# Attention layers on one core: the Sync engine's order, with the read-back of q and k behind the second row of maxima

## Chip, core and metric

The kernel runs on one core of a Trainium2 chip. The metric is the device time of one launch in microseconds (us). TensorE is the matrix engine (PE; PEld is its weight load), VectorE is DVE, ScalarE is ACT, GpSimd is POOL, and SyncE is SP (SPq in the trace: its instruction queue), which here only issues DMAs.

## What is computed

Two layers, each: group norm of x (64 samples of 14 x 14 tokens and 192 channels, 32 groups), then attention with 12 heads of 16 channels and a relative position bias that depends on q, then a projection, added to x.

```python
x = x + _L0_conv_ref(_gn(x), ...)
x = x + _L1_conv_ref(_gn(x), ...)
# each layer, with B = 64 samples, nh = 12, hd = 16, HW = 196:
qkv = hidden.reshape(B, HW, C) @ W + b
attn = einsum('bqd,bkd->bqk', q * scale, k)
rel_h = einsum('bhwc,hkc->bhwk', q, Rh)
rel_w = einsum('bhwc,wkc->bhwk', q, Rw)
attn = softmax(attn + rel_h[..., None] + rel_w[..., None, :])
out = einsum('bqk,bkd->bqd', attn, v) @ proj + b
```

## The kernel before

One sample of one layer is a unit; there are 128 (2 x 64). The kernel is one software pipeline over units. Every engine runs the same loop: iteration i has 12 slots, and a table gives each piece of work a number "at". A piece with number `at` belongs, in iteration i, to unit i - at // 12 and stands in slot at % 12. Within a slot the order is that of the code. The tables are `JOBS` (TensorE's jobs), `POOL_AT` and `SP_AT`; `due` (with `head_at` for the heads) picks the unit. A number therefore sets two things: the unit lag, and the place in the engine's instruction order. All waits are semaphore waits ahead of the instruction, so an engine's queue stands still behind one that waits.

Per unit: x is loaded (xa), transposed, normalised, q, k and v are made (jobs qk0, qk1 in slot 3, v in slot 10). q and k go in two halves (high and low part in f16) to DRAM (L341, `to_dram`) and are read back in another layout: q to q_st (L369), k to k_st in two DMAs (L375). q_st and k_st hold a stack of rows over which one matmul contracts: q and k rows, rows of the relative bias (rel_hl, written by four DMAs of L358), and one last row with minus the maximum of each query. For that row, TensorE first computes all scores once (L525, into ps_max), VectorE reduces them to maxima (L722), TensorE transposes six heads' maxima at a time (jobs mT0, mT1), ScalarE copies them to mrow (L610), and a DMA of the Sync engine puts each half into the last row of q_st (L336, `maxima`; half 0 is called m0, half 1 m1). Then the scores are computed again with the row in them (L538, into ps_sc; head 0 needs m0, head 6 needs m1), ScalarE takes the exponential, the product with v follows (L557, with the sum of the softmax in it), then the transposition, division and projection. ScalarE makes yr from the projection (L657), GpSimd adds the input (L862: yo = yr + xd), and the Sync engine writes it out (L387). xd is loaded by the Sync engine (L382).

The heads' scores: `MAX_AT` is 28 and `EXP_AT` is 40, one head a slot. So head 0 of the second scores stands in slot 4, head 6 in slot 10. The transposition mT0 is at 35 (slot 11), mT1 at 41 (slot 5); ScalarE copies mrow one slot later (slots 0 and 6). The relative bias is made by jobs rel0 to rel2 at 17, 18 and 20. GpSimd's `POOL_AT` has mv at -11 (slot 1) ahead of y at 63 (slot 3), and mv waits for VectorE's statistics, which stand in slot 5.

The Sync engine's order in one iteration, from `SP_AT` before: slot 0 xa (L394); slot 3 m0 (L336), q and k to DRAM (L341 twice, waits for VectorE's low part of q and k), q read back (L369, waits until q has landed in DRAM); slot 4 k read back (L375 twice, waits until k has landed); slot 7 xd (L382, waits for the yo of the unit before its own); slot 9 output (L387, waits for its own yo); slot 10 m1 (L336, waits for mrow) and the relative bias (L358 four times, waits for VectorE's rel_hl, L776).

```python
wait(sp, s_mrow, unit_.n * 2 + half + 1)   # maxima: m0, m1
wait_dma(sp, s_qd, u)                      # q_in
wait_dma(sp, s_kd, u)                      # k_in
wait(sp, s_y, u.n - 1)                     # xd
wait(sp, s_y, u.n + 1)                     # out
```

Of the kernel before, what the change touches and what calls it, by code (L numbers as in the profile page):

```python
# [71 lines left out]
def attention_kernel(nc, x_in, w_all, b_qk, b_rows, rel, onehot, lo_rows, ident_in, gmat_in, out):  # L72
    with ExitStack() as ctx:
# [41 lines left out]
        def pair(name, shape, dt=F32):  # L115
            return [sb(f"{name}{i}", shape, dt) for i in range(2)]

        xa = pair("xa", [HT, 2, C])
# [25 lines left out]
        xd = pair("xd", [HT, 2, C])  # L144
# [126 lines left out]
        POOL_AT = {"mv": -11, "group": -3, "xn": -1, "xhi": 0, "xlo": 0, "y": 63}  # L271
        QK_TILES = ((0, 1), (2,))

        SP_AT = {"m0": 39, "m1": 46, "rel": 22, "qk_out": 3, "q_in": 3, "k_in": 4, "xd": 55, "out": 69, "xa": -12}

        def head_at(base, slot):

# [2 lines left out]
        def due(unit, slot, at):  # L280

            u = unit(at // HEADS)
            return u if at % HEADS == slot and active(u) else None
# [24 lines left out]
        def _(sp):  # L308
# [23 lines left out]
            def maxima(unit_, half):  # L332

                if active(unit_):
                    wait(sp, s_mrow, unit_.n * 2 + half + 1)
                    sp.dma_start(q_st[unit_.r][R_MAX:STACK, half * HH:half * HH + HH, :, :],  # L336
                                 mrow[unit_.r % 2][:, half, :]).then_inc(s_m[half][unit_.r], 16)

            def to_dram(unit_, dram, row, landed):

                sp.dma_start(dram[unit_.r].rearrange("l d h c t -> (d h) l (c t)"),  # L341
                             qk_hl[unit_.r % 2][row:row + HQ * HD, :, :, :]
                             .rearrange("p l c t -> p l (c t)")).then_inc(landed[unit_.r], 16)

            def iteration(unit, layer):
                for s in range(HEADS):
                    for half in range(2):
                        u = due(unit, s, SP_AT[f"m{half}"])
                        if u:
                            maxima(u, half)  # L350
                    u = due(unit, s, SP_AT["rel"])
                    if u:
                        wait(sp, s_rlo, u.n * 3 + 3)
                        for axis in range(2):
                            rows = RW if axis == 0 else 2 * SIDE
                            for half in range(2):
                                p, r0 = 64 * axis + 32 * half, R_REL + RW * axis
                                sp.dma_start(q_st[u.r][r0:r0 + rows, half * HH:half * HH + HH, :, :],  # L358
                                             rel_hl[u.r % 2][p:p + rows, :, :]).then_inc(s_rel[u.r], 16)
                    u = due(unit, s, SP_AT["qk_out"])  # L360
                    if u:
                        wait(sp, s_qklo, u.n * 2 + 2)
                        to_dram(u, q_dram, 0, s_qd)
                        to_dram(u, k_dram, HQ * HD, s_kd)
                    u = due(unit, s, SP_AT["q_in"])
                    if u:
# [3 lines left out]
                          .then_inc(s_qst[u.r], 16)  # L370
                    u = due(unit, s, SP_AT["k_in"])
                    if u:
                        wait_dma(sp, s_kd, u)
                        for part in range(2):
                            sp.dma_start(k_st[u.r][2 * HD * part:2 * HD * part + 2 * HD, :, :],  # L375
                                         k_dram[u.r].rearrange("l d h c t -> d l (h c t)"))\
                              .then_inc(s_kst[u.r], 16)
                    u = due(unit, s, SP_AT["xd"])
                    if u:
# [541 lines left out]
```

## Time and profile before

| | |
|---|---|
| median of 3 runs | 2342.62 us (2330.44 to 2347.41) |
| profiled execution | 2339.97 us, span 2338.2 us |
| mean granted TensorE clock | 0.978 of full |
| busy: PE, PEld | 90%, 68% of the span |
| busy: DVE, ACT, POOL | 71%, 69%, 31% |
| DMA | 216 MB, mean 93 GB/s, 37.7% of the 16 engines' time on the Sync engine's queue |
| chain that ended last | PE 39%, DMA 33% (of it q_st<-mrow 17%, k_dram<-qk_hl 10%, q_dram<-qk_hl 6%), SP's queue 14% |

Busy means that an instruction runs; for TensorE the ends of matmuls are modelled. The chain is followed back from the last instruction through whatever released each step. A wait in the list of waits stands as "who waited <- for whom: us in total, times, longest".

### The profile page before, as it was taken

The page shows a single profiled execution, that of the slowest core. Times are in us where ns is not written, and L with a number is a line of the kernel's source. Part 1 is how long each engine was busy: PE and PEld are TensorE (multiplying, and loading weights), DVE is VectorE, ACT ScalarE, POOL GpSimd, SP SyncE. Part 2 cuts the span into 40 slices and gives each one's busy share as a digit, 9 for nine tenths or more (in the row PEclk, how much of TensorE's full clock was granted, in tenths as well). Part 3 has the DMA queues.
Part 4 walks back from the last instruction along what each step waited for, and adds up shares of the span by engine and source line. Part 5 has one row for each costly group of instructions (what it writes and reads, how often), then busy time and mean ns, then how long its engine had stood idle before and what let it go on. Part 6 is the DMA issues. An engine that isn't in the chain of part 4 may idle for free.

```text
span 2338.2 us, 73485 instructions
## 1 busy us (share of the span) xinstructions
PE 2094.7 (90%) x27904; PEld 1595.9 (68%) x27904; DVE 1653.4 (71%) x3923; ACT 1621.4 (69%) x3713; POOL 714.4 (31%) x1796
## 2 busy tenths in 40 slices
PE   1899999999999989999999999899989999999998
PEld 1677676776767767667667766677766766777765
DVE  5677777667767677777677777677767777777675
ACT  0577777677767667767676777677767776777675
POOL 1233323333333233333233333233223333333230
PEclk9899999999999999999999999999999999999999
DMA  1333434333434333433333443344334343334331
GB/s 47 84 94 95 104 91 105 91 92 91 103 93 97 90 94 93 101 93 93 91 98 91 94 103 96 88 96 100 91 91 102 94 100 93 94 93 103 91 92 47
DMA packets 170550, 216.34 MB, mean 93 GB/s; under 512 B 29783, under 2 KB 138072, under 8 KB 170202
## 3 DMA queue, kind: packets, MB, share of 16 engines
q1 hardware_dynamic: 170202, 211.64, 37.7%
q8 instruction: 226, 3.70, 0.7%
q14 instruction: 122, 1.00, 0.2%
HBM read 117.00 MB, written 57.80 MB: 75 GB/s over the span
## 4 chain that ended last, share of the span: by engine, by line
PE 39%; DMA 33%; SPq 14%; DVE 6%; issue 4%; ACT 3%; POOL 1%; POOLq 0%; ACTq 0%; DVEq 0%
PE ps_m L412 18%; DMA q_st<-mrow 17%; DMA k_dram<-qk_hl 10%; PE ps_sc L538 7%; PE ps_max L525 6%; SPq L375 6%; DMA q_dram<-qk_hl 6%; DVE qk_hl L734 4%; PE ps_o L557 3%; SPq L382 3%; ACT qk_hl L598 2%; SPq L341 2%; SPq L387 2%; PE ps_m L501 2%; DVE rel_hl L776 1%
## 5 line engine op out<-in xcount | busy, mean ns | idle before, releaser
L722 DVE TENSOR_REDUCE mx<-ps_max 98x2 f32<-98x392 f32 x1536 | 819.4, 562 | 232.6 <-PE ps_max L525 215.5
L586 ACT ACTIVATE probs<-ps_sc 98x392 f32<-98x392 f32 x1536 | 714.5, 497 | 232.3 <-PE ps_sc L538 198.2
L525 PE MATMUL ps_max<-k_st,q_st 124*98 124x196 f16 x3072 | 548.9, 261 | 82.4 <-DVE mx L722 82.1
L538 PE MATMUL ps_sc<-q_st,k_st 125*98 125x196 f16 x3072 | 523.3, 252 | 95.6 <-DMA q_st<-mrow 94.1
L776 DVE TENSOR_TENSOR rel_hl<-ps_m,rel_hi 64x504 f16<-64x504 f32 (+1 forms) x768 | 431.4, 562 | 162.0 <-ACT rel_hi L643 152.9
L525 PEld LDWEIGHTS ps_max<-k_st,q_st 124*98 124x98 f16 x3072 | 295.0, 126 | 296.4 <-issue 198.0
L538 PEld LDWEIGHTS ps_sc<-q_st,k_st 125*98 125x98 f16 x3072 | 320.9, 126 | 123.1 <-DMA q_st<-mrow 120.4
L557 PE MATMUL ps_o<-probs,v_st 98*32 98x196 f32 x6144 | 389.6, 340 | 0.5 <-ACT o_sb L578 0.5
L634 ACT ACTIVATE rel_hi<-ps_m,is_lo 64x504 f16<-64x504 f32 (+1 forms) x384 | 223.9, 583 | 189.1 <-PE ps_m L471 185.7
L471 PE MATMUL ps_m<-q_st,rel_st 64*32 64x84 f16 x7168 | 341.6, 266 | 4.8 <-DVE rel_hl L776 4.5
L809 POOL TENSOR_TENSOR msq<-mv 96x2 f32<-96x2 f32 x128 | 24.4, 191 | 1007.1 <-DVE mv L748 1007.1
L643 ACT ACTIVATE rel_hi<-ps_m,is_lo 64x504 f16<-64x504 f32 (+1 forms) x384 | 226.0, 589 | 4.7
L471 PEld LDWEIGHTS ps_m<-q_st,rel_st 64*32 64x32 f16 x7168 | 174.9, 99 | 76.4 <-DVE rel_hl L776 5.1
L557 PEld LDWEIGHTS ps_o<-probs,v_st 98*32 98x32 f32 x6144 | 134.4, 108 | 135.6 <-issue 74.9
L734 DVE TENSOR_TENSOR qk_hl<-ps_m,qk_hl 128x392 f16<-128x392 f32 (+1 forms) x256 | 107.1, 459 | 149.3 <-ACT qk_hl L598 149.3
L412 PE MATMUL ps_m<-xn_hi,w_hi 98*128 98x196 f16 (+1 forms) x768 | 193.5, 252 | 10.5 <-POOL xn_lo L851 10.5
L412 PE MATMUL ps_m<-xn_lo,w_hi 96*128 96x196 f16 x768 | 192.3, 250 | 0.0
L412 PE MATMUL ps_m<-xn_hi,w_lo 96*128 96x196 f16 x768 | 191.7, 250 | 0.0
L819 POOL TENSOR_TENSOR msq<-gsm 96x2 f32<-96x2 f32 x128 | 24.6, 192 | 481.7 <-DVE gsm L791 481.7
L598 ACT CAST qk_hl<-ps_m 128x392 f16<-128x392 f32 (+1 forms) x256 | 103.6, 405 | 86.5 <-PE ps_m L412 83.3
L491 PE MATMUL ps_m<-ident,o_sb 128*98 128x68 f32 x1536 | 151.7, 247 | 0.4 <-ACT o_sb L578 0.4
L862 POOL TENSOR_TENSOR yo<-yr,xd 98x384 f32<-98x384 f32 x128 | 128.0, 1000 | 60.5 <-ACT yr L657 60.5
(72 smaller groups left out, 3293.8 us busy)
## 6 DMA issues: line engine op xcount, KB each, us to landing
q_st<-q_dram SPq DMA_DIRECT2D x128, 294.0 KB, 3.8
k_st<-k_dram SPq DMA_DIRECT2D x256, 147.0 KB, 3.9
q_dram<-qk_hl SPq DMA_DIRECT2D x128, 147.0 KB, 2.6
k_dram<-qk_hl SPq DMA_DIRECT2D x128, 147.0 KB, 2.7
q_st<-rel_hl SPq DMA_DIRECT2D x256, 73.5 KB
q_st<-rel_hl SPq DMA_DIRECT2D x256, 64.3 KB
xa<-in_x SPq DMA_DIRECT2D x64, 147.0 KB
xd<-in_x SPq DMA_DIRECT2D x64, 147.0 KB
```

The lines of the kernel that those rows point to most:

```text
L412: last = nc.tensor.matmul(dst, weights(a, c, k), moving(b, c, k), start=n == 0, stop=n == len(terms) - 1)
L471: last = nc.tensor.matmul(to, rel_st[:, lay, axis, w:w + RW], q[:, :, a * SIDE:a * SIDE + SIDE] if axis == 0 else q[:, :, a::SIDE], start= ...
L491: last = nc.tensor.matmul(ps[0:HT, at:at + HG * (HD + 1)], o_sb[p2][:, g, h * HT:h * HT + HT], ident[:, :].rearrange("p (j x) -> p j x", x ...
L525: last = nc.tensor.matmul(ps_max[head % 2][0:HT, h * TOK:h * TOK + TOK], q_st[u.r][0:R_MAX, head, h, :], k_st[u.r][0:R_MAX, head, :], star ...
L538: last = nc.tensor.matmul(ps_sc[head % 2][0:HT, kt * TOK:kt * TOK + TOK], k_st[u.r][0:STACK, head, kt * HT:kt * HT + HT], q_st[u.r][0:STAC ...
L557: last = nc.tensor.matmul(ps_o[32 * j:32 * j + 32, 0:TOK], v_st[u.r][:, kt, head_of(head), :], p[:, kt, :], start=kt == 0, stop=kt == 1)
L586: nc.scalar.activation(probs[head][:, :, :], ps_sc[head % 2][0:HT, 0:2 * TOK].rearrange("p (k t) -> p k t", k=2), ACT.Exp, scale=1.0 / (QS ...
L634: nc.scalar.activation(dst, src, ACT.Identity, scale=is_lo[0:64, 0:1])
L643: nc.scalar.activation(dst, src, ACT.Identity, scale=is_lo[64:128, 0:1])\
L722: nc.vector.reduce_max(mx[u.r % 2][:, head, :], ps_max[head % 2][0:HT, 0:2 * TOK].rearrange("p (q k) -> p q k", q=2), axis=AX.X).then_inc( ...
L734: nc.vector.tensor_tensor(qk_hl[u.r % 2][:, 1, at, :], ps_m[BANK[f"qk{j}"]][:, 0:len(tiles) * TOK].rearrange("p (c t) -> p c t", t=TOK), q ...
L776: last = nc.vector.tensor_tensor(l, src, h, ALU.subtract)
```

## The change

Only the numbers of the Sync engine's table change. The unit lag (number // 12) stays the same for all of them; the slot changes.

```diff
-        SP_AT = {"m0": 39, "m1": 46, "rel": 22, "qk_out": 3, "q_in": 3, "k_in": 4, "xd": 55, "out": 69, "xa": -12}
+        SP_AT = {"m0": 37, "m1": 43, "rel": 22, "qk_out": 4, "q_in": 8, "k_in": 8, "xd": 54, "out": 66, "xa": -12}
```

Order of one iteration before: xa | m0, q and k to DRAM, q read back, k read back twice | xd | output | m1, relative bias. After: xa | m0 | q and k to DRAM | xd, output | m1 | q read back, k read back twice | relative bias.

## Rows read from the trace of the kernel before

**Rows 1.** The page: engine, busy us (share of the span), instructions.

```profile
PE 2094.7 (90%) x27904; PEld 1595.9 (68%) x27904; DVE 1653.4 (71%) x3923; ACT 1621.4 (69%) x3713; POOL 714.4 (31%) x1796
```

**Rows 2.** Waits of the whole span: who <- for whom: us, times, longest us.

```profile
PEld ps_sc L538 <- DMA q_st<-mrow: 120.4, 123, 2.3
PE ps_sc L538 <- DMA q_st<-mrow: 94.1, 105, 2.1
PE ps_max L525 <- DVE mx L722: 82.1, 130, 1.6
```

**Rows 3.** Windows: stretch, length, busy us of each engine, granted clock, DMA share, GB/s.

```profile
147.80:164.34 16.54, 15.90 (x222) 12.12 (x220) 12.65 (x31) 12.61 (x29) 5.58 (x14) 1.00 0.39 102
164.34:180.97 16.63, 15.95 (x222) 12.08 (x219) 12.68 (x31) 12.62 (x29) 5.59 (x14) 1.00 0.42 101
...
2135.68:2152.25 16.57, 15.96 (x224) 12.21 (x220) 12.71 (x32) 12.68 (x30) 5.57 (x14) 1.00 0.43 102
847.33:867.41 20.08, 17.50 (x222) 13.71 (x220) 12.77 (x31) 12.83 (x29) 5.59 (x14) 0.92 0.35 83
...
858.40:861.81 3.41, 3.41 (x24) 3.38 (x22) 1.48 (x3) 1.60 (x4) 0.00 (x0) 0.50 0.24 63
110.66:2276.16 2165.50, 1993.43 (x26817) 1520.97 (x26814) 1560.44 (x3690) 1555.85 (x3566) 686.11 (x1722) 0.98 0.40 95
```

**Rows 4.** Timeline of the Sync engine, one unit: start us, us, line, out<-in.

```profile
163.70 0.64 SPq L341 DMA_DIRECT2D k_dram<-qk_hl  x1
165.64 0.56 SPq L369 DMA_DIRECT2D q_st<-q_dram  x1
166.30 1.22 SPq L375 DMA_DIRECT2D k_st<-k_dram  x2
167.57 0.57 SPq L382 DMA_DIRECT2D xd<-in_x  x1
168.18 0.41 SPq L387 DMA_DIRECT2D x<-yo  x1
168.64 0.82 SPq L336 DMA_DIRECT2D q_st<-mrow  x1
172.21 2.88 SPq L358 DMA_DIRECT2D q_st<-rel_hl  x4
...
175.74 0.73 SPq L336 DMA_DIRECT2D q_st<-mrow  x1
```

**Rows 5.** Second row of maxima: landings (chain), and issue and use (timeline).

```profile
168.64 3.32 DMA q_st<-mrow
...
203.09 2.25 DMA q_st<-mrow
...
851.72 0.82 SPq L336 DMA_DIRECT2D q_st<-mrow  x1
...
856.88 0.37 PE L538 MATMUL ps_sc<-q_st,k_st 125*98 125x196 f16 x2 [1.96 <-DMA q_st<-mrow]
```

**Rows 6.** Waits of the Sync engine's queue over the whole span.

```profile
SPq L369 <- DMA q_dram<-qk_hl: 198.6, 128, 2.9
...
SPq L375 <- DMA k_dram<-qk_hl: 43.3, 38, 2.1
```

**Rows 7.** Timelines of POOL, ACT and PE in the unit of rows 4.

```profile
165.56 1.00 POOL L862 TENSOR_TENSOR yo<-yr,xd 98x384 f32<-98x384 f32 x1
...
166.54 0.23 ACT L610 ACTIVATE mrow<-ps_m 12x98 f16<-12x98 f32 x1
...
179.65 0.33 PE L538 MATMUL ps_sc<-q_st,k_st 125*98 125x196 f16 x2
```

**Rows 8.** DMA issues: out<-in, count, KB each, median us to landing.

```profile
q_st<-q_dram SPq DMA_DIRECT2D x128, 294.0 KB, 3.8
k_st<-k_dram SPq DMA_DIRECT2D x256, 147.0 KB, 3.9
```

**Rows 9.** The chain, first row of maxima in the tail: start us, us.

```profile
2287.41 3.31 DMA q_st<-mrow
```

## The prediction

> **What bounds the kernel now.** I read the page first: TensorE is busy 2094.7 us of 2338.2 [rows 1], so nothing but TensorE's own gaps and its own pace can be won. Then the waits: what TensorE waits for is the row of maxima. Weight loads of L538 wait 120.4 us for it, matmuls of L538 94.1 us in 105 waits; the next wait is 82.1 us for the reductions of L722 [rows 2]. The matmul figure is the one that counts as lost, because a weight load may wait while the matmul before it still runs.
>
> Then the windows. I measure a unit from the end of its k_dram issue (called T) to the next one. From T = 110.66 to T = 2276.16 there are 123 units in 2165.50 us, 17.61 us each [rows 3]. But a unit in which the matmuls do not wait takes 16.54, 16.63 or 16.57 us (three windows of some twenty such units, which lie between 16.49 and 16.96; two of the three follow each other) [rows 3]. A unit that does wait is longer by its wait and sometimes by more: the one from 847.33 takes 20.08 us with a wait of 1.96 us [rows 3, 5]. The rest, 20.08 - 1.96 - 16.59 = 1.53 us, is the clock: right behind the wait there is a stretch of 3.41 us with a granted clock of 0.50, the 1.2 GHz level [rows 3].
>
> So the sum over the 123 units closes: 2165.5 = 123 x 16.59 (2040.6) + 94.1 of waits + 30.8 of half clock. I take 16.59, which is within 0.01 of the mean of the three windows (16.58). All but 0.58 us of the 94.1 lies in these units.
>
> Last, the Sync engine's order in a unit without a wait [rows 4], T = 163.70 + 0.64 = 164.34. It waits for q to land in DRAM (read-back at T+1.30, and over the run 198.6 us, 1.55 us a unit, are spent in that wait [rows 6]), then issues q, twice k, xd, output, and only at T+4.30 the second row of maxima (m1). That row had been ready since 166.54 + 0.23 = T+2.43 [rows 7]. It lands 3.32 us after its issue [rows 5], T+7.62. When does TensorE want it? In the unit from 847.33 the matmul starts at 856.88 after waiting 1.96 us: from T+7.59 [rows 5]. So even the good unit makes it with nothing to spare, and any late landing of q or k in DRAM (k_dram has its own wait, 38 times, up to 2.1 us [rows 6]) is paid by TensorE in full.
>
> **The change, part by part.** Slots mean order only: the Sync engine does nothing else. m0 goes from slot 3 to 1, but stays between xa and the write-out of q and k: no cost, no gain. The unit lags are the same, every instruction is still issued once, so no bytes and no issues are added. What really moves is the read-back of q and k (three issues) from ahead of xd, output and m1 to behind them.
>
> xd and output: both wait for the sum of the unit before (yo). It ends at 165.56 + 1.00 = T+2.22 [rows 7]. Before, this was always past; now it is the wait that ends last, and m1 stands behind it. That is a wait that takes the removed one's place, but it ends 0.21 us ahead of the maxima's own readiness. xd then costs 0.57, output 0.41, with gaps 1.07 us together [rows 4], so m1 is issued at T+3.3 in place of T+4.3, and in the bad units in place of T+5 to T+6.3, since neither landing in DRAM stands ahead of it any more.
>
> m1's landing with the new neighbours is not in this trace. Bounds: 2.25 us is the shortest, 5.16 us (851.72 to 856.88) the longest [rows 5]. Landings near the long end had q, two k, xd and output (882 KB) issued within 3 us ahead; now it is xd and output, 294 KB, behind q and k writes that are mostly done. I take the middle one, 3.32, as it is the safe side of what fewer bytes should give: landing at T+6.6, 1.0 us ahead of the need. It stays free of a wait up to a landing of 7.59 - 3.3 = 4.3 us. The Trainium skill (DMA: Bandwidth & Descriptors, "Queues, rings and completion order") says that the semaphore increment of a DMA lands only after all earlier writes of its DMA engine, and ("Anatomy of one DMA") fits a DMA as 2.0 us plus bytes at 436 GB/s. By an estimate from that page 882 KB ahead would be 4.1 us and 294 KB 2.7 us; the trace's 3.3 to 5.2 for the former agrees roughly, the latter no run of before shows.
>
> q and k read-back: issued from T+4.2 to T+6.1 (0.56 + 1.22 us and m1's 0.82 [rows 4]). q is used in the next unit (rel0, slot 5 of it, over 10 us later) and lands in 3.8 us; k lands in 3.9 us [rows 8], T+9.4, used two units later: free. The rel rows are issued at T+7.87 [rows 4], when their data is ready, and the queue is free 1.8 us before: free. xa and m0 stay behind rel: m0 at T+11.40 [rows 4]. Its cover is thinner: the first matmul that needs it starts at 179.65 = T+15.31 [rows 7], 3.91 us after the issue, and in the quiet tail it landed in 3.31 us [rows 9].
>
> The sum: -94 us of waits. The half clock stretches come right behind such waits, so they go with them: -31 us. Added: 0. On the execution's own 2339.97 us (span 2338.2 and 1.8 around it): 2340 - 125 = 2215 us; the median of the three runs, 2342.6, is 2.6 above this execution, within their scatter, and I leave it. A base of 16.50 or 16.70 us a unit in place of 16.59 gives 2204 or 2229. I say 2214.
>
> **The rivals.**
> 1. m0 becomes the late one (slower). q and k are now read 3 us later and so closer to rel and m0. The skill's rule above speaks for it: increments behind unfinished writes land late. If m0 took 5.16 us, the longest seen, it would be late by 1.25 us a unit, 154 us, and the half clock would stay: 2215 + 154 + 31 = 2400. It decides from 4.7 us on: 3.91 + (125 - 31)/123. Against it: k lands by T+9.4, 2 us before m0 is issued. 3 in 100.
> 2. m1 still lands late, say in 4.6 us, between the middle and the longest of the three landings [rows 5]: late by 4.6 - 4.3 = 0.3, 123 x 0.3 = 37 us, 2252. Speaks for it: landings vary by 2.9 us in this trace. Against: the bytes that made it late are behind it now. 7 in 100.
> 3. The waits go but the clock still falls (other gaps are left, 82.1 us for L722 [rows 2]): 2215 + 31 = 2246. Against: the units without a wait have clock 1.00. 5 in 100.
> 4. The order changes and nothing comes of it, because another wait of TensorE grows by the 1.0 us that is taken out (the reductions no longer get that pause to catch up): 2340. Against: units without the wait follow each other at 16.6 us. 3 in 100.
>
> **How the numbers follow.** The forecast has 82 in 100, own range 2204 to 2229. With rival 3 and the mild half of rival 2 the range goes to 2248; below, 2200. A difference of 1% (23 us) is about what a measurement of this kernel can tell from none. Rival 1 is slower (0.03), rival 4 the same (0.03), all others faster (0.94).
>
> **What would show it.** Right: the Sync engine no longer waits at q_dram for any length, m1 issued at T+3.3, no wait of L538 for the row of maxima, units of 16.6 us throughout, clock 1.00 in the steady part. Wrong: waits of L538 in the slot of head 0 (m0, rival 1) or head 6 at T+7.6 (rival 2); half clock without such waits (rival 3); L722 waits well over 82 us (rival 4). The forecast as a whole falls if the yo sum ends later than T+3.3, because then xd holds m1 as q_dram did.

## The result and the profile after

| | before | after |
|---|---|---|
| median | 2342.18 us (2330.44 to 2347.41) | 2196.20 us (2192.44 to 2200.86) |
| ratio, 95% interval | | 0.9384 (0.9343 to 0.9425) |
| profiled execution, span | 2338.2 us | 2196.7 us |
| mean granted TensorE clock | 0.978 | 0.996 |

The change makes the kernel 146 us faster. That is 4 us below the low end of the range, and 18 us below the predicted time.

The waits of the kernel after, those that answer to [rows 2] and [rows 6]: who waits for whom, us, times, longest.

```profile
PEld ps_max L525 <- DVE mx L722: 98.2, 139, 1.8
PE ps_max L525 <- DVE mx L722: 82.6, 130, 1.8
...
PEld ps_m L429 <- DMA xa<-in_x: 6.6, 15, 1.2
...
PEld ps_m L429 <- DMA xa<-x: 6.1, 13, 0.9
...
PEld ps_sc L538 <- DMA q_st<-mrow: 3.4, 6, 0.9
...
PE ps_sc L538 <- DMA q_st<-mrow: 2.2, 5, 0.7
```

```profile
SPq L387 <- POOL yo L862: 211.0, 126, 8.9
...
SPq L369 <- DMA q_dram<-qk_hl: 5.6, 3, 2.9
SPq L382 <- POOL yo L862: 1.1, 1, 1.1
```

The wait for the second row of maxima is gone: head 6 does not wait in any unit, and the 2.2 us that are left (94.1 before) are those of head 0, for m0. The wait for the reductions stands at 82.6 as before at 82.1. What has grown is the wait for xa: weight loads wait 12.7 us for it (6.6 + 6.1), where they waited 1.9 before. On the Sync engine the wait for q landing in DRAM (198.6) has become one for yo, 211.0 us. It is the output (L387) that has it, not xd (L382, one wait), and it costs TensorE nothing as long as m1 behind it is in time.

One unit in the Sync engine's timeline, to be held against [rows 4]; T = 173.44 + 0.64 = 174.08:

```profile
173.44 0.64 SPq L341 DMA_DIRECT2D k_dram<-qk_hl  x1
174.13 0.58 SPq L382 DMA_DIRECT2D xd<-in_x  x1
176.34 0.33 SPq L387 DMA_DIRECT2D x<-yo  x1
176.71 0.79 SPq L336 DMA_DIRECT2D q_st<-mrow  x1
177.54 0.58 SPq L369 DMA_DIRECT2D q_st<-q_dram  x1
178.16 1.23 SPq L375 DMA_DIRECT2D k_st<-k_dram  x2
181.96 2.87 SPq L358 DMA_DIRECT2D q_st<-rel_hl  x4
184.88 1.44 SPq L394 DMA_DIRECT2D xa<-in_x  x1
```

m1 is issued at T+2.63, 0.4 us behind the end of the sum yo that the output waits for; it was at T+4.30 in a good unit before.

Windows: that unit, and the 123 units together (columns as in [rows 3]).

```profile
174.08:190.44 16.36, 15.62 (x218) 11.85 (x216) 12.27 (x30) 12.34 (x29) 5.57 (x14) 1.00 0.41 103
...
108.31:2136.66 2028.35, 1942.14 (x26817) 1486.61 (x26814) 1549.40 (x3690) 1549.55 (x3566) 684.81 (x1722) 1.00 0.42 102
```

The 123 units take 2028.35 us in place of 2165.50: 137 us of the 141.5 by which the span is shorter. The usual unit takes 16.36 us. None of the 123 units before was that short: the shortest took 16.50, the three good ones in [rows 3] 16.54 to 16.63.

### The profile page after: what moved, and what is told of

It reads as the page before. It is cut to its first block, busy times and chain, and to the rows that moved or that the text cites. A ratio compares the mean times of both kernels' runs of the same rounds, so it can differ in the third digit from the quotient of the medians.

```text
span 2196.7 us, 73485 instructions
## 1 busy us (share of the span) xinstructions
PE 2039.4 (93%) x27904; PEld 1558.4 (71%) x27904; DVE 1641.9 (75%) x3923; ACT 1614.9 (74%) x3713; POOL 713.0 (32%) x1796
## 2 busy tenths in 40 slices
DMA packets 170550, 216.34 MB, mean 98 GB/s; under 512 B 29783, under 2 KB 138072, under 8 KB 170202
## 4 chain that ended last, share of the span: by engine, by line
PE 61%; DVE 18%; issue 7%; DMA 5%; ACT 4%; SPq 4%; POOL 1%; ACTq 0%; DVEq 0%; POOLq 0%
PE ps_m L412 16%; PE ps_max L525 11%; DVE rel_hl L776 11%; PE ps_o L557 9%; PE ps_sc L538 8%; PE ps_m L471 8%; DVE mx L722 5%; PE ps_m L491 4%; ACT rel_hi L643 4%; SPq L358 4%; PE ps_m L429 2%; DMA xa<-in_x 2%; DMA xa<-x 2%; PE ps_m L501 1%; DMA q_st<-mrow 1%
## 5 line engine op out<-in xcount | busy, mean ns | idle before, releaser
L525 PE MATMUL ps_max<-k_st,q_st 124*98 124x196 f16 x3072 | 541.8, 258 | 83.5 <-DVE mx L722 82.6
L538 PE MATMUL ps_sc<-q_st,k_st 125*98 125x196 f16 x3072 | 512.0, 247 | 2.5 <-DMA q_st<-mrow 2.2
L525 PEld LDWEIGHTS ps_max<-k_st,q_st 124*98 124x98 f16 x3072 | 289.3, 124 | 296.6 <-issue 197.3
```

Source lines behind the costliest of these rows:

```text
L525: last = nc.tensor.matmul(ps_max[head % 2][0:HT, h * TOK:h * TOK + TOK], q_st[u.r][0:R_MAX, head, h, :], k_st[u.r][0:R_MAX, head, :], star ...
L538: last = nc.tensor.matmul(ps_sc[head % 2][0:HT, kt * TOK:kt * TOK + TOK], k_st[u.r][0:STACK, head, kt * HT:kt * HT + HT], q_st[u.r][0:STAC ...
```

## The unit that seemed to wait for nothing

Where are those 0.2 us a unit? TensorE's timeline around head 6, first of before, in the good unit from 164.34, then of after, in the unit from 174.08. The last two rows of the first fence are the weight loads of the same stretch.

```profile
171.56 0.37 PE L525 MATMUL ps_max<-k_st,q_st 124*98 124x196 f16 x2
172.01 0.37 PE L538 MATMUL ps_sc<-q_st,k_st 125*98 125x196 f16 x2
...
171.56 0.17 PEld L525 LDWEIGHTS ps_max<-k_st,q_st 124*98 124x98 f16 x2 [0.31 <-issue]
172.00 0.17 PEld L538 LDWEIGHTS ps_sc<-q_st,k_st 125*98 125x98 f16 x2 [0.28 <-DMA q_st<-mrow]
```

```profile
181.31 0.37 PE L525 MATMUL ps_max<-k_st,q_st 124*98 124x196 f16 x2
181.52 0.33 PE L538 MATMUL ps_sc<-q_st,k_st 125*98 125x196 f16 x2
```

From the start of the first pair to the start of the second it is 0.45 us before and 0.21 after. The good unit lost 0.24 us to the row of maxima, and its matmul shows no wait: the modelled end of the matmul before (171.56 + 0.37) covers most of the gap. Only the weight load shows it. The deadline read as T+7.59 was late by 0.15 us for the same reason: free, the matmul starts at T+7.44.

The same distance can be taken at head 6 in all 123 units of before. It is above 0.21 us in every one of them (by 0.02 us in the best, by 0.9 in the median), and the excess comes to 113.5 us, where the matmuls' listed waits come to 93.5. So 20 us of lost time, 0.16 us a unit, are in no listed wait. After, the excess at head 6 is zero in all 123 units.

## Experiments

T is always the end of the k_dram issue, and "the 123 units" are those from the fifth k_dram issue to the last. Each edit is against the changed kernel; the diffs show only the entries of `SP_AT` that change.

**Read-backs ahead of m1, without a wait for DRAM.**

```diff
-"m1": 43, "q_in": 8, "k_in": 8
+"m1": 44, "q_in": 7, "k_in": 7
```

> The changed kernel with the read-back of q and k put back ahead of the second row of maxima (m1), but behind xd and output, so that no wait for q or k landing in DRAM stands ahead of m1: only three issues (1.8 us) and 588 KB do. Order: q and k to DRAM, xd, output, q back, k back twice, m1, relative bias. T is the end of the k_dram issue. Theory A (a unit costs 16.36 us, and more only by what m1 lands after about T+7.4): m1 is issued at T+4.5 and lands 3.3 to 4.6 us later, late by 0.4 to 1.7 us a unit, mean about 0.75: units of 17.1 us, 2290 us (2250 to 2340). Rival B (it was the wait for the landing in DRAM alone that cost): within 10 us of the changed kernel, 2200.

Measured: 2288.1 us, ratio to before 0.9794 (0.9756 to 0.9833). One unit, first the Sync engine's rows, then TensorE's, then its window; T = 178.31.

```profile
180.93 0.56 SPq L369 DMA_DIRECT2D q_st<-q_dram  x1
181.54 1.23 SPq L375 DMA_DIRECT2D k_st<-k_dram  x2
182.81 0.81 SPq L336 DMA_DIRECT2D q_st<-mrow  x1
...
185.57 0.37 PE L525 MATMUL ps_max<-k_st,q_st 124*98 124x196 f16 x2
186.31 0.37 PE L538 MATMUL ps_sc<-q_st,k_st 125*98 125x196 f16 x2 [0.36 <-DMA q_st<-mrow]
```

```profile
178.31:195.27 16.96, 15.97 (x222) 12.12 (x220) 12.68 (x31) 12.61 (x29) 5.59 (x14) 1.00 0.40 98
```

m1 is issued at T+4.50 and the matmul starts at T+8.00. Start to start it is 0.74 us where 0.21 is free: 0.53 lost, of which the wait listed is 0.36. The unit is 0.60 longer than 16.36. So each listed wait leaves out about 0.16 us. Over the run the listed waits of these matmuls are 69.7 us, and the 123 units take 2120.05 us, 107.8 above 123 x 16.36: 89 of them are the excess from start to start at head 6, and about 10 are lost in six units with 3.41 us of half clock each. Theory A holds and rival B falls: of the 146 us, about 90 come from putting the read-backs behind m1. The other 50 or so are left for no longer waiting for DRAM ahead of it and for the rest of the order; no run separates these two.

**m1 first, xd and output last.**

```diff
-"m1": 43, "q_in": 8, "k_in": 8, "xd": 54, "out": 66
+"m1": 41, "q_in": 6, "k_in": 6, "xd": 55, "out": 69
```

> The changed kernel with m1 ahead of xd and output and these two last: q and k to DRAM, m1, q back, k back twice, xd, output, relative bias. m1 then waits only for its own data and is issued at T+2.45. Theory A: m1 had 1 us or more to spare already, so nothing is won: 2190 to 2205 us. Rival C (xd and output going early is part of the gain): 2220 us or more.

Measured: 2200.97 us (2200.62 to 2201.57). Moving xd and output ahead of m1 is no part of the gain; m1 at T+2.47 in place of T+2.63 wins nothing.

**q ahead of m1, k behind it.**

```diff
-"m1": 43, "q_in": 8, "k_in": 8
+"m1": 44, "q_in": 7, "k_in": 9
```

> The changed kernel with q's read-back alone ahead of m1, k's two behind it. m1 is issued at T+3.2 with 294 KB more ahead of it. Theory A (the deadline is T+7.4, and lateness under 0.15 us or so is paid though no wait of the matmuls is listed): m1 lands 3.0 to 4.3 us after its issue, T+6.2 to T+7.5, so nearly all units take 16.36 us, 2200 us (2190 to 2225), and those that take 16.4 to 16.6 us show a wait of the weight load alone. Rival F (a unit of this kernel takes 16.5 to 16.6 us whenever a read-back stands ahead of m1, whether m1 is late or not): 2215 to 2225 us with no weight load waiting.

Measured: 2201.42 us (2199.19 to 2202.75). m1 is issued at T+3.24 in the usual unit, that unit takes 16.36 us, and the waits of the weight load for the row of maxima are 3.9 us in 7 times. Rival F falls. With one read-back ahead of it m1 is issued at T+3.2 and is free; with all three ahead it is issued at T+4.5 and costs 0.2 us at least, 0.6 in the median unit. The next run shows that T+4.5 by itself is not too late.

**The same order as rb_before_m1, with a twelfth of the bytes.**

The diff is shortened: `as rows` stands for the same view as before.

```diff
 # on top of rb_before_m1; q_st and k_st rows set to zero once at the start
-sp.dma_start(q_st[u.r][0:R_REL, :, :, :], q_part.to_broadcast([2 * HD, 2, HEADS * TOK]))
+sp.dma_start(q_st[u.r][0:R_REL, 0:1, :, :], q_part[:, :, 0:TOK].to_broadcast([2 * HD, 2, TOK]))
-sp.dma_start(k_st[u.r][rows, :, :], k_dram[u.r] as rows)
+sp.dma_start(k_st[u.r][rows, 0:1, :], k_dram[u.r] as rows, head 0 alone)
```

> The order of rb_before_m1 (q and k read back ahead of m1), but each of the three read-backs moves one head of the twelve: 49 KB in place of 588 KB, with the same three issues. The other heads' q and k rows stay zero (set once at the start, a few us), so the attention of eleven heads is left out. Theory G (m1 lands late because its increment comes behind the bytes issued ahead of it): m1 is issued at T+4.0 to T+4.5 and lands in 2.3 to 2.9 us, before T+7.4; units of 16.4 us, no wait for the row of maxima. Rival H (the place in the queue and the three issues alone make it late): units of 17.0 to 17.2 us and waits of 60 us and more, as in rb_before_m1.

Measured in one execution: 2217.8 us, with a start that is about 12 us longer (the zeros). The kernel leaves out the attention of eleven heads. Its Sync engine, T = 186.69, the unit's window, and its waits:

```profile
189.32 0.57 SPq L369 DMA_DIRECT2D q_st<-q_dram  x1
189.93 1.23 SPq L375 DMA_DIRECT2D k_st<-k_dram  x2
191.20 0.81 SPq L336 DMA_DIRECT2D q_st<-mrow  x1
```

```profile
186.69:203.05 16.36, 15.74 (x222) 12.09 (x220) 12.60 (x31) 12.61 (x29) 5.59 (x14) 1.00 0.29 68
```

```profile
PEld ps_m L429 <- DMA xa<-x: 7.7, 17, 0.8
...
PEld ps_m L429 <- DMA xa<-in_x: 6.8, 17, 1.1
...
PE ps_sc L538 <- DMA q_st<-mrow: 4.4, 8, 1.1
```

The same three issues, m1 at the same T+4.51, and the unit takes 16.36 us; the waits fall from 69.7 to 4.4 us. It is the bytes ahead of m1 that made it land late, not its place in the queue or the issues' time. The number of DMA packets is the same in both runs, 170550, so it is not their count either.

The landing itself can be read from the increments of m1's semaphore in each trace (the last one counted; it agrees with the 3.32 of [rows 5]). Over the 123 units, in us:

| | m1 issued, median | issue to landing: median (least to most) | time lost at head 6 |
|---|---|---|---|
| before | T+4.81 | 3.39 (2.18 to 5.12) | 113.5 |
| rb_before_m1 | T+4.51 | 3.41 (2.67 to 4.83) | 89.1 |
| q_before_m1 | T+3.25 | 3.56 (2.84 to 4.98) | 1.5 |
| rb_before_m1_thin | T+4.65 | 1.92 (1.88 to 3.59) | 2.6 |
| after | T+2.64 | 1.90 (1.86 to 3.40) | 0 |

A full read-back right ahead of m1 adds 1.5 us to its landing, and one of 294 KB does it as much as all three with 588 KB.

The landings agree with the rule that the prediction drew on (the Trainium skill, DMA: Bandwidth & Descriptors, "Queues, rings and completion order": the increment lands after all earlier writes of its DMA engine). The weight loads' waits for xa, however, are as large as in the changed kernel (14.5 us against 12.7): the read-backs' bytes do not cause them.

**xa earlier.** What the changed kernel's 123 units take above 123 x 16.36 is 16 us, and weight loads wait 12.7 us for xa. Here xa goes right behind m1. That takes it out from in front of m0 too, which is issued at T+10.8 in place of T+11.4.

```diff
-LEAD, TAIL = 1, 6
+LEAD, TAIL = 2, 6
-"xa": -12
+"xa": -17
```

> The changed kernel with the load xa issued ahead of the read-backs (slot 7 of the iteration before, in place of slot 0 behind the relative bias; one more empty iteration at the start). Theory D (what the changed kernel's units take above 16.36 us, 17 us in all over 123 units, is xa landing late behind the read-backs: weight loads of L429 wait 12.7 us for it): 2183 us, units of 16.36 us throughout, no wait of L429 for xa. Rival E (the rest is scatter of other kinds): 2196 us as the changed kernel.

Measured: 2190.44 us. One of its four executions took 9604.89 us, which no other one of any kernel did and which stays unexplained; the other three lie between 2186.54 and 2190.77. The profile has no wait for xa, but one unit of 21.17 us, and half clock in it:

```profile
343.84 0.52 PE L525 MATMUL ps_max<-k_st,q_st 124*98 124x196 f16 x2 [0.98 <-DVE mx L722]
...
339.57:360.74 21.17, 20.19 (x222) 15.83 (x220) 13.05 (x31) 13.01 (x29) 5.59 (x14) 0.76 0.33 80
344.00:354.20 10.20, 10.20 (x74) 8.30 (x74) 6.27 (x15) 4.22 (x10) 4.24 (x11) 0.50 0.41 102
```

So both kernels were run again, side by side on one chip, six executions each.

> The changed kernel again, beside the version with xa early on the same chip. Every theory: 2192 to 2201 us.

> The version with xa ahead of the read-backs again, on the same chip as the changed kernel. Theory D (late xa is what the changed kernel has above 16.36 us a unit): 8 to 14 us under the changed kernel, about 2184 us; the single unit of 21.2 us of the first run is not there again. Rival E: within 3 us of the changed kernel.

Measured: the changed kernel 2200.12 us (2197.36 to 2201.97, six executions), with xa early 2186.57 us (2183.24 to 2190.29, six). The ranges do not meet: 13.6 us, 0.6%. The units of the latter:

```profile
191.97:208.35 16.38, 15.74 (x222) 12.13 (x220) 12.60 (x31) 12.62 (x29) 5.59 (x14) 1.00 0.42 102
110.15:2123.57 2013.42, 1936.18 (x26817) 1488.63 (x26814) 1548.66 (x3690) 1551.37 (x3566) 687.57 (x1722) 1.00 0.42 102
```

2013.42 is 123 x 16.37: the units are at the floor, and no wait for xa or for a row of maxima is listed. The unit of 21.17 us is not there. Theory D holds for the most part. Not all of the gain is xa's: in the changed kernel m0 is late six times as well, which costs 3 us from start to start, and that goes too, since m0 is issued earlier here.

> xa ahead of the read-backs, and m1 ahead of xd and output too. Theory A: m1 lands 1 us or more before it is needed in either place, so the time is that of xa_early, 2184 us, within 5 us. If m1 still waits now and then: 2 to 4 us less.

With m1 first as well (`"xa": -17, "m1": 41`): 2187.51 us, the same. No wait of TensorE for a DMA is listed in this run, so of these waits there is nothing left to win by the Sync engine's order.

**Read-backs further back, ahead of xa and m0.**

```diff
-"q_in": 8, "k_in": 8
+"q_in": 10, "k_in": 10
```

> The changed kernel with the read-backs moved further, behind the relative bias, right ahead of xa and m0. This makes the rival of the prediction in which the first row of maxima (m0) and xa become late: m0 is issued near T+13.2 in place of T+11.4 and is needed at T+15.1, xa near T+12.7. Theory A: lateness is paid in full, 2 to 3 us a unit, and half clock comes back: 2450 to 2600 us, slower than the kernel before. If m0 and xa had more room than the 3.7 us seen, under 2300 us.

Measured in one execution: 2709.9 us, mean clock 0.854. Waits, then one unit:

```profile
PE ps_m L429 <- DMA xa<-in_x: 148.2, 55, 4.1
PE ps_m L429 <- DMA xa<-x: 122.2, 51, 3.7
...
PE ps_sc L538 <- DMA q_st<-mrow: 4.5, 2, 3.3
```

```profile
267.95 2.92 SPq L358 DMA_DIRECT2D q_st<-rel_hl  x4
270.91 0.61 SPq L369 DMA_DIRECT2D q_st<-q_dram  x1
271.56 1.25 SPq L375 DMA_DIRECT2D k_st<-k_dram  x2
272.86 0.56 SPq L394 DMA_DIRECT2D xa<-in_x  x1
```

The order that hurts is slower than before, as expected, and by more (2450 to 2600 was said). It is xa that is late, 270 us of waits; m0, behind it in the queue, is hardly listed (4.5 us), since TensorE already stands at xa. With it comes the half clock: a mean of 0.854 is 29% of the span at half clock ((1 - 0.854) x 2).

## Why the prediction was off

**Right.** The mechanism and the signs named for it: the wait for the row of maxima goes (94.1 to 2.2 us), the half clock of the steady part goes with it (71.7 us at 0.50 in 17 of the 123 units before, none after), and no wait that a rival named grows by more than 3 us. m1 had a large reserve: it lands at T+4.6 in the median, 2.9 us ahead of its use, and q_before_m1 issues it 0.6 us later for nothing. The relative bias stayed in time, m0 but for 3 us in all. Rival 4 (the reductions as the next bound) did not come: 82.6 us against 82.1. Rival 3 did not either; in rb_before_m1, 117 of the 123 units keep clock 1.00, the middle half of all with listed gaps of 0.3 to 0.7 us.

**Wrong: the base of the sum.** "I take 16.59" for a unit without a wait was mis-sized; it is 16.36, and 123 x 0.23 = 28 us are missing from the gain. The prediction saw the sign of it: that the good unit "makes it with nothing to spare", and that weight loads wait 120.4 us where matmuls wait 94.1. It dropped the larger figure because a load may wait while a matmul still runs. Of the 26 us between them 20 were real time. The shown shortest unit was taken for a unit free of the effect, when every unit had some of it. The closing sum (2040.6 + 94.1 + 30.8) was no check: 30.8 is what that base leaves over. With the right floor the same 2165.5 us are 2012.3, and 93.5 of listed waits at head 6, 20 unlisted there, 33.5 that the 17 units with half clock take beyond their late start, and 6 spread over the rest. Most of the missing 28 us is thus the unlisted part.

**Wrong, without effect on the time:** the step that let xd wait for yo of the same iteration. xd is of unit i-4 and waits for the count of the sum one iteration back; it goes at T+0.05. (The description of the kernel before has it wait for the unit before its own; `wait(sp, s_y, u.n - 1)` asks for the one before that.) Only the output waits. m1 therefore went at T+2.63 and not at T+3.3. The run q_before_m1, with m1 at T+3.2, shows that T+3.3 would have been as good. The landing was off too: 3.32 us was assumed, 1.90 is the median. The prediction's other figure, 2.7 us, comes from a fit that the Trainium skill (DMA: Bandwidth & Descriptors, "Anatomy of one DMA — SWDGE (gpsimd) path") gives for DMAs issued from GpSimd, while m1 is issued from the Sync engine; and of the 294 KB that it counts ahead of m1, xd's half was issued 2.6 us before. The bounds of 2.25 and 5.16 us came from units with the same five transfers issued ahead of m1. At 1.90 us m1 is in time with much room, so the time did not hang on this.

**Missing:** xa. The changed kernel pays 16 us above the floor: 11 from start to start for xa landing late in 29 of the 123 units, 3 for m0, and 2 spread. I had looked for a late m0 and passed over xa in front of it, which is issued 0.6 us earlier and used 1.1 us earlier. In the unit from 164.34 of before it is issued at 175.14 and its first transposition starts at 178.54, 3.40 us later, where m0 has 3.91. The waits of the whole span below are also of before:

```profile
175.14 0.55 SPq L394 DMA_DIRECT2D xa<-in_x  x1
178.54 0.50 PE L429 MATMUL ps_m<-ident,xa 98*96 98x98 f32 x4
...
PE ps_m L429 <- DMA xa<-in_x: 0.5, 1, 0.5
PE ps_m L429 <- DMA xa<-x: 0.2, 1, 0.2
```

Before, the late head 6 held TensorE back in the same unit and hid it (0.7 us of listed matmul waits for xa before, 5.9 after). The traces bear that out: xa is issued and lands as before (median T+10.9, then 2.5 us in both), but in the median unit its landing is 1.2 us ahead of its use before and 0.6 after. The thin run excludes the moved read-backs as its cause.

The sum with measured terms, for the 123 units: -93.5 listed, -20 unlisted, -33.5 with the half clock, -6 spread, +16 for xa, m0 and the rest = -137; measured -137.2. Start and tail give another 4. So two errors partly cancelled: the base alone hid 28 us of gain, and 16 us came back as late xa and m0 that the prediction had at zero. That the miss is 18 us and not over 30 is luck.

## What to carry to other kernels

A small transfer that gates the busiest engine belongs ahead of the large ones in its queue; here read-backs issued right in front of 2.3 KB made it land in 3.4 us in place of 1.9 (medians), and with a twelfth of the bytes the same order cost next to nothing. To find the floor of a repeating unit, do not trust the best unit of a profile in which the same wait may touch every one: compare start-to-start distances around the suspected wait, and look at the weight loads' waits as well (they list somewhat too much: 118 us at head 6 for 113.5 lost). When one wait is removed, the next one in the order of time is often one that it had been hiding; look for what is used next behind it, not only for what was moved.

## What was unexpected of the hardware

The listed wait of a late matmul was 0.16 us shorter than the time lost by it (0.36 listed, 0.53 lost in the unit shown; 0 listed and 0.24 lost in another, since gaps up to 0.15 us are not listed at all).

How long a wait was does not tell whether the clock falls. Before, the 17 units with half clock had gaps of 0.93 to 2.13 us at head 6, but others kept clock 1.00 with gaps up to 1.72. In rb_before_m1 six units fell after gaps of 1.08 to 1.78 us, and others kept 1.00 with up to 1.70.

Once, in xa_early, the clock fell to 0.50 for 10.2 us in a unit with no wait for a DMA at all; it cost 4.8 us. It fell right behind the wait for the reductions, which is 0.98 us in that unit and 0.61 to 0.64 in all others. But the changed kernel (0.98 us) and xa_early_again (0.99 us) have the same long wait in the same place and keep clock 1.00. The cause is open.
